# Gated cross-attention block on one core: token and attention-output tiles transposed by DMA instead of TensorE

## The chip, the cores and the metric

The kernel runs on one core of a Trainium2 chip. The metric is the time of the device in microseconds for one execution. A core has the engines PE (TensorE), DVE (VectorE), ACT (ScalarE), POOL (GpSimd) and SP (SyncE); each works through its own instructions in order, and semaphores tie them together.

## The reference

Two batches of 2048 tokens with 512 features go through gated cross-attention (16 heads of 32 features, 77 context positions) and a gated feed-forward block with fake-quantised activations and weights (hidden size 1408):

```python
q = (layernorm(x) @ Wq)                      # heads of 32
scores = q @ k.T * scale ; attn = softmax(scores)
x = x + tanh(g_xattn[0]) * ((attn @ v) @ Wo)
xq = act_fake_quant(layernorm(x), clip_x)    # needs max |layernorm(x)| over all tokens
h  = act_fake_quant(silu(xq @ wg) * (xq @ wu), clip_down)
x = x + tanh(g_ffn[0]) * (h @ wd)
```

Only the attention part is touched here.

## The kernel before

The 4096 tokens are 32 tiles of 128 (NT = 32), held in `x1`. The kernel has three blocks one after the other: attention (up to about 406 us), "up" and "down". In the attention block all engines walk the same slots n = 0 to 35 (`tile_slots`, L326), and in a slot several tiles at different steps are in hand. Slots 4 to 19 are a hardware loop, the rest is written out. Every engine's work stands in a fixed order written out by hand in its `slot`, and only semaphores tie the engines together, so an instruction that waits holds up all that stands behind it on its engine.

Tile m is handled in this order:

- POOL's `deviation` (L423) turns mean and variance into scale and bias; ACT's `normalise` (L494) writes the normalised tile `xn` (one buffer).
- PE's `x_transpose` (L885) turns `xn` into `p_x` with four 128x128 f32 transposes. ACT copies the high part to `xT_hi` (L503), DVE the rest to `xT_lo` (L611).
- PE's `queries` (L892) and `scores` (L912, two halves). DVE takes the row maximum (L633) and subtracts it into `prob` (L639); this write of half 0 is called the first subtraction here, that of half 1 the second. ACT takes the exponential (L531). `prob` has two buffers, for even and odd tiles, with 616 f32 elements in each half.
- PE transposes the probabilities in three groups (L937), ACT copies each group (L527), PE multiplies with the values (L948), DVE divides by the sum into `o_sb` (L652), half by half.
- In slot m+2 PE's `out_transpose` (L963) turns `o_sb` into `p_x` with four transposes, ACT and DVE split it into `oT_hi` (L515) and `oT_lo` (L662), and at the end of the slot `project` (L974) multiplies with Wo into `p_y`, DVE adds to `x1` in slot m+3 (L730) and takes statistics. In slot m+4 ACT writes the absolute value of the second layernorm to `xabs` (L522), and DVE takes its maximum (L782).

Beside this runs the preparation of the feed-forward weights: in slots 0 to 21 one row block a slot is loaded by SP (`rows`, L349), DVE takes its maximum (L753), scales it to int8 (L771), POOL casts it to bf16 (L458), and SP issues one DMA transpose of 128x512 two-byte elements (`rows_transposed`, L344). From slot 22 on the down weights go a similar way.

PE's order in slot n, for the steps that matter: scores half 0 of tile n, `out_transpose(n-2)`, eight probability transposes of tile n-1, queries, outputs half 0, scores half 1, two probability transposes, queries, outputs half 1, `x_transpose(n+4)`, `project(n-2)`. ACT ends its slot with the exponential of half 1, the copy to `xT_hi` of tile n+4, and `normalise(n+5)`.

## Time and profile before

| | us |
|---|---|
| median of 3 runs | 651.65 (651.65 to 651.79) |
| the profiled execution | 651.6 |
| its span from first to last instruction | 649.6 |

The profile comes from one execution. "Busy" counts an instruction from its start to its end; instructions of one engine overlap a little, so the distance from one start to the next (called the pitch here) is what the engine's order costs. Line numbers are those of the kernel before.

### The profile page before, as it was taken

The page shows a single profiled execution, that of the slowest core. Times are in us where ns is not written, and L with a number is a line of the kernel's source. Part 1 is how long each engine was busy: PE and PEld are TensorE (multiplying, and loading weights), DVE is VectorE, ACT ScalarE, POOL GpSimd, SP SyncE. Part 2 cuts the span into 40 slices and gives each one's busy share as a digit, 9 for nine tenths or more (in the row PEclk, how much of TensorE's full clock was granted, in tenths as well). Part 3 has the DMA queues.
Part 4 walks back from the last instruction along what each step waited for, and adds up shares of the span by engine and source line. Part 5 has one row for each costly group of instructions (what it writes and reads, how often), then busy time and mean ns, then how long its engine had stood idle before and what let it go on. Part 6 is the DMA issues. An engine that isn't in the chain of part 4 may idle for free. (4 is left out here: it accounts for less than half of the span.)

```text
span 649.6 us, 12819 instructions
## 1 busy us (share of the span) xinstructions
PE 629.0 (97%) x3987; PEld 478.6 (74%) x4008; DVE 505.3 (78%) x954; ACT 319.8 (49%) x488; POOL 174.5 (27%) x392
## 2 busy tenths in 40 slices
PE   8969999999999999999999997899999999899997
PEld 6769999999999999999999997444444444344544
DVE  6686878788787887888888766688888888876764
ACT  4354544445444554544544432555555554365653
POOL 7121223223232222212212111111111110047775
PEclk9999999999999999999999999899999999999999
DMA  8639111101111011011112000058465110089723
GB/s 308 189 95 318 47 28 26 49 24 48 24 29 44 25 48 25 28 52 62 29 47 68 18 7 0 18 174 192 161 210 202 31 28 17 0 291 413 292 105 128
DMA packets 59861, 63.32 MB, mean 97 GB/s; under 512 B 39571, under 2 KB 42029, under 8 KB 59821
## 3 DMA queue, kind: packets, MB, share of 16 engines
q1 hardware_dynamic: 54915, 46.03, 23.7%
q10 hardware_dynamic: 4906, 16.78, 7.0%
q8 instruction: 22, 0.36, 0.2%
q14 instruction: 18, 0.15, 0.1%
HBM read 32.48 MB, written 21.36 MB: 83 GB/s over the span
## 5 line engine op out<-in xcount | busy, mean ns | idle before, releaser
L633 DVE TENSOR_REDUCE sb_smax<-ps_s 128x8 f32<-128x616 f32 x64 | 51.1, 799 | 59.4 <-PE ps_s L926 59.0
L1231 ACT ACTIVATE sb_silu<-ps_g,sb_sgu 128x512 f32<-128x512 f32 x88 | 60.5, 687 | 72.1 <-PE ps_g L1318 43.8
L1318 PE MATMUL ps_g<-sb_xqT,sb_wgu 128*128 128x512 bf16 x344 | 89.3, 379 | 1.0 <-DVE sb_xqT L1274 0.6
L1318 PE MATMUL ps_u<-sb_xqT,sb_wgu 128*128 128x512 bf16 x346 | 89.4, 379 | 0.3
L527 ACT COPY sb_pT<-ps_p 128x512 f32<-128x512 f32 (+1 forms) x96 | 46.5, 520 | 71.5 <-PE ps_p L937 71.5
L1289 DVE SCALAR_TENSOR_TENSOR sb_h<-ps_u,sb_sgu,sb_silu 128x512 f32<-128x512 f32 (+1 forms) x88 | 66.1, 751 | 19.4 <-PE ps_u L1318 18.8
L948 PE MATMUL ps_o<-sb_vblk,sb_pT 128*128 (+4 forms) x640 | 79.0, 270 | 1.2 <-ACT sb_pT L527 1.2
L948 PEld LDWEIGHTS ps_o<-sb_vblk,sb_pT 128*128 128x128 f32 (+1 forms) x640 | 76.8, 191 | 1.8 <-ACT sb_pT L527 1.4
L881 PE MATMUL ps_q<-sb_xT_hi,sb_wq_hi 128*128 128x256 f32 x256 | 78.0, 305 | 0.0
L882 PE MATMUL ps_q<-sb_xT_lo,sb_wq_hi 128*128 128x256 f32 x256 | 72.6, 284 | 0.0
L883 PE MATMUL ps_q<-sb_xT_hi,sb_wq_lo 128*128 128x256 f32 x256 | 72.6, 284 | 0.0
L1524 PE MATMUL ps_z<-sb_wdT,sb_hq 128*128 128x512 bf16 x324 | 71.2, 379 | 0.3
L1399 POOL TENSOR_TENSOR sb_wgu<-sb_wgu,sb_x 128x512 f32<-128x512 f32 x31 | 53.4, 1723 | 52.3 <-DVE sb_wgu L1456 52.0
L1293 DVE TENSOR_REDUCE sb_hmax<-sb_h 128x1 f32<-128x512 f32 (+1 forms) x88 | 60.4, 686 | 8.0 <-DVE sb_h L1289 0.7
L1318 PEld LDWEIGHTS ps_g<-sb_xqT,sb_wgu 128*128 128x128 bf16 x352 | 34.4, 98 | 42.1 <-ACT sb_xqT L1245 0.8
L1318 PEld LDWEIGHTS ps_u<-sb_xqT,sb_wgu 128*128 128x128 bf16 x352 | 34.4, 98 | 41.5
L515 ACT CAST sb_oT_hi<-ps_x 128x512 fp32r<-128x512 f32 x31 | 18.2, 587 | 90.2 <-PE ps_x L971 90.2
L1524 PEld LDWEIGHTS ps_z<-sb_wdT,sb_hq 128*128 128x128 bf16 x330 | 32.2, 98 | 39.0 <-ACT sb_hq L1416 0.5
L1419 ACT CAST sb_hq<-sb_h 128x1408 bf16<-128x1408 int8 (+1 forms) x32 | 42.0, 1312 | 27.5 <-DVE sb_h L1449 23.6
L639 DVE TENSOR_TENSOR sb_prob<-ps_s,sb_smax 128x616 f32<-128x616 f32 x64 | 51.0, 796 | 2.7
L440 POOL TENSOR_TENSOR sb_ve<-sb_mvt,sb_eps 128x1 f32<-128x1 f32 x32 | 6.1, 190 | 172.1 <-DVE sb_mvt L757 170.3
L881 PE MATMUL ps_y<-sb_wo_hi,sb_oT_hi 128*128 128x512 f32 x124 | 51.3, 414 | 0.0
(212 smaller groups left out, 1351.8 us busy)
## 6 DMA issues: line engine op xcount, KB each, us to landing
h_spill<-sb_h SPq DMA_DIRECT2D x4, 2816.0 KB, 8.9
sb_h<-h_spill ACTq DMA_DIRECT2D x16, 704.0 KB, 7.5
out_dram<-sb_wgu SPq DMA_DIRECT2D x31, 256.0 KB, 2.1
sb_x<-in_x_dram ACTq DMA_DIRECT2D x1, 4096.0 KB, 16.8
sb_w_in<-in_L_ffn_w_gate_dram SPq DMA_DIRECT2D x11, 256.0 KB, 2.6
sb_w_in<-in_L_ffn_w_up_dram SPq DMA_DIRECT2D x11, 256.0 KB, 2.6
sb_x<-in_x_dram SPq DMA_DIRECT2D x2, 1024.0 KB, 14.7
sb_x<-in_x_dram SPq DMA_DIRECT2D x2, 512.0 KB, 5.3
```

Source lines behind the costliest of these rows:

```text
L633: dve.tensor_reduce(smax[:, half, :].rearrange("p (g h) -> p g h", g=2), half_scores(), X, ALU.max).then_inc(v_max, 1)
L639: dve.tensor_tensor(prob[t % 2][:, half, :].rearrange("p (g h m) -> p g h m", g=2, h=HG), half_scores(), smax[:, half, :].rearrange("p (g ...
L881: pe.matmul(o, hi, rhi, start=first, stop=False)
L882: pe.matmul(o, hi, rlo, start=False, stop=False)
L883: return pe.matmul(o, lo, rhi, start=False, stop=last)
L948: last = pe.matmul(p_o[:, first:end + 1, :].rearrange("p h d -> p (h d)"), pT[rows, half * KB + j, :], vblk[rows, span(b), half, SLOT0[j]: ...
L1231: act.activation(silu[(j * KI + i) % 2][:, :, :].rearrange("p t n -> p (t n)"), p_g[(j * KI + i) % 2][:, :], ACT.Silu, scale=sgu[:, i:i + ...
L1289: dve.scalar_tensor_tensor(steps_h, p_u[(j * KI + i) % 2][:, :, :], sgu[:, KI + i:KI + i + 1], silu[(j * KI + i) % 2][:, :, :], ALU.mult, ...
L1293: dve.tensor_reduce(hmax[:, span(u)], steps_h, mybir.AxisListType.XY, ALU.max, apply_absolute_value=True).then_inc(v_hmax, 1)
L1318: last = pe.matmul(banks[(j * KI + i) % 2][:, :], wgu[:, what, k, i * P:(i + 1) * P], xqT[j][:, k, :], start=(k == 0), stop=(k == KD - 1))
L1399: pool.tensor_tensor(yd[k], yd[k], x1[:, span((v + RT) % NT), :].rearrange("p a d -> p (a d)"), ALU.add).then_inc(g_out, 1)
L1524: last = pe.matmul(p_z[k % 4][:, :], hq[k % 4][:, i, :], wdT[:, i, :], start=(i == 0), stop=(i == KI - 1))
```

## The change

Tiles 8 to 31 of the normalised tokens and tiles 2 to 29 of the attention output are no longer transposed by PE. POOL splits each f32 tile, seen as pairs of 16-bit halves, into a plane of low and a plane of high halves; SP transposes the planes by DMA (two-byte elements); ACT joins the transposed planes into f32 words in a buffer `xpl`, and copies from there to the high part. The planes are written into `prob`, which is idle for that time: those of the token tile in half 1, those of the output in half 0. So the next subtraction into a half of `prob` waits until the DMA that reads its planes has landed. `xabs` moves to the PSUM bank of `p_y` for most tiles, because `xpl` takes its place, and `project` waits for its maximum. DVE's order within a slot is changed. Some semaphores are shared between blocks to make room for the new ones.

```diff
@@ SP: once a slot
+                    def planes_transposed(n):
+                        sp.wait_ge(g_xpl, n - DIRECT + 1)
+                        sp.dma_start_transpose(xn_u[:, :].rearrange("p (c n) -> p c n", n=P),
+                                               x_planes(n)).then_inc(d_xT, 16)
+                    def out_transposed(m, half):
+                        sp.wait_ge(g_opl, 2 * (m - O_FIRST) + half + 1)
+                        sp.dma_start_transpose(o_pairs(half).rearrange("p (c n) -> p c n", n=P),
+                                               o_planes(m, half)).then_inc(d_oT, 16)
+                    def slot_transposes(n):
+                        if o_joined(n - 2):
+                            out_transposed(n - 2, 1)
+                        if DIRECT <= n + 4 < NT:
+                            planes_transposed(n + 4)
+                        if o_joined(n - 1):
+                            out_transposed(n - 1, 0)
@@ POOL
+                    def x_split(t):
+                        pool.tensor_copy(x_planes(t).rearrange("p (two n) -> p two n", two=2), xn_pairs)\
+                            .then_inc(g_xpl, 1)
+                    def out_split(t, half):
+                        pool.tensor_copy(o_planes(t, half).rearrange("p (two n) -> p two n", two=2),
+                                         o_pairs(half).rearrange("p (n two) -> p two n", two=2)).then_inc(g_opl, 1)
+                    def deviation(n, t, x_ready=False, o_ready=False):
                         wait(pool, v_st, n + 1)
                         wait(pool, g_nb, n)
-                        wait(pool, a_xn, n - 1)
+                        if x_ready:
+                            wait(pool, a_xn, n)
+                            wait(pool, t_p, 3 * (n - 6))
...
+                        if o_ready:
+                            wait(pool, v_o, 2 * (n - 6))
                         pool.tensor_tensor(ve[:, :], mv[:, 1:2], eps[:, :], ALU.add).then_inc(g_self, 1)
                         pool.tensor_tensor(nmean[:, :], mv[:, 0:1], minus[:, :], ALU.mult).then_inc(g_self, 1)
+                        if o_ready:
+                            out_split(t - 7, 1)
+                        if x_ready:
+                            x_split(t - 1)
                         wait(pool, g_self, 3 * n + 2)
...
-                    def deviation2(m):
+                    def deviation2(m, t):
...
+                        if o_joined(m + 2):
+                            wait(pool, v_o, 2 * (m + 2) + 1)
+                            wait(pool, t_p, 3 * (m + 2) + 2)
                         pool.tensor_tensor(nb2[:, span(m)], nmean2[:, :], rs2[:, span(m)], ALU.mult)\
                             .then_inc(g_nb2, 1)
+                        if o_joined(m + 2):
+                            out_split(t + 2, 0)
@@ ACT
+                            wait(act, a_xpl, n - DIRECT)          # normalise
+                    def out_join(m):
+                        wait(act, d_oT, 32 * (m - O_FIRST + 1))
+                        wait(act, v_xlo, min(m + 6, NT) if isinstance(m, int) else m + 6)
+                        act.copy(xpl_halves, o_halves).then_inc(a_opl, 1)
+                        wait(act, a_opl, m - O_FIRST + 1)
+                        wait(act, t_y, m)
+                        act.copy(oT(m)[0], xpl_T).then_inc(a_ohi, 1)
+                    def x_join(n, t):
+                        wait(act, d_xT, (n - DIRECT) * 16 + 16)
+                        wait(act, v_olo, n - 5)
+                        act.copy(xpl_pairs, xn_planes).then_inc(a_xpl, 1)
+                        wait(act, a_xpl, n - DIRECT + 1)
+                        wait(act, t_q, n - t % 2 - 2)
+                        act.copy(xT_hi[t // 2][:, :, t % 2 * P:(t % 2 + 1) * P], xpl_T).then_inc(a_xhi, 1)
...
                         for c, (k0, k1) in enumerate(CHUNKS):
+                            if c == 2 and runs(n - 2, NT) and o_joined(n - 2):
+                                out_join(n - 2)
...
+                            if half == 0 and runs(n - 4, NT - 1):     # between the two exponentials
...
+                                act.activation(xabs(n - 4), row(n - 4), ACT.Abs, bias=nb2[:, span(n - 4)],
+                                               scale=rs2[:, span(n - 4)]).then_inc(a_abs, 1)
@@ DVE
+                        if half == 0 and o_joined(n - 2):             # in scores_sub
+                            wait(dve, d_oT, 32 * (n - 1 - O_FIRST))
+                        if half == 1 and runs(n + 4, NT) and joined(n + 4):
+                            wait(dve, d_xT, 16 * (n + 5 - DIRECT))
@@ PE
+                        if not isinstance(m, int) or m < PLANES_FREE - 2:   # project
+                            wait(pe, v_xmax, m)
-                        if runs(n - 2, NT - 1):
+                        if runs(n - 2, NT - 1) and not o_joined(n - 2):
                             out_transpose(n - 2)
-                        if runs(n + 4, NT):
+                        if not joined(n + 4):
                             wait(pe, v_olo, n - 1)
                             x_transpose(n + 4)
```

(`DIRECT` is 8, `O_FIRST, O_END` are 2 and 30; the remarks behind # stand for the function that the line is in.) DVE's new order in slot n is: maximum half 0, add to `x1`, maximum of the weight rows, first subtraction, statistics, reciprocal, division half 0, `out_part(n-2)` (the write of `oT_lo`), maximum half 1, int8 scaling, maximum of `xabs`, second subtraction, then as before but with `stats_end` ahead of `x_part`. Before, the write of `oT_lo` and the weight maximum stood between the statistics and the reciprocal, and the maximum of `xabs` behind the second subtraction.

## Rows read from the trace of the kernel before

**Rows 1.** The page, its head and part 1 (busy us, share of span, instructions)

```profile
span 649.6 us, 12819 instructions
...
PE 629.0 (97%) x3987; PEld 478.6 (74%) x4008; DVE 505.3 (78%) x954; ACT 319.8 (49%) x488; POOL 174.5 (27%) x392
```

**Rows 2.** Busy time by stretch: us, busy per engine, PEclk, DMA share, GB/s

```profile
200.00:300.00 100.00, 100.00 (x753) 95.59 (x752) 83.74 (x180) 51.29 (x89) 25.78 (x84) 1.00 0.12 34
```

**Rows 3.** Timeline of PE around slot 16: start us, us, operation

```profile
206.11 0.60 PE L889 MATMUL ps_x<-sb_identf,sb_xn 128*128 128x128 f32 x4
206.47 0.48 PE L881 MATMUL ps_y<-sb_wo_hi,sb_oT_hi 128*128 128x512 f32 x1
...
209.33 0.30 PE L924 MATMUL ps_s<-sb_k_hi,sb_q_hi 128*128 x1
...
210.18 0.60 PE L971 MATMUL ps_x<-sb_identf,sb_o_sb 128*128 128x128 f32 x4
210.61 1.04 PE L937 MATMUL ps_p<-sb_identf,sb_prob 128*128 128x128 f32 x8
...
213.95 0.39 PE L924 MATMUL ps_s<-sb_k_hi,sb_q_hi 128*128 x1
...
220.83 0.30 PE L924 MATMUL ps_s<-sb_k_hi,sb_q_hi 128*128 x1
```

**Rows 4.** Timeline of DVE in slot 16

```profile
211.92 0.80 DVE L639 TENSOR_TENSOR sb_prob<-ps_s,sb_smax 128x616 f32<-128x616 f32 x1
...
213.23 0.68 DVE L662 TENSOR_TENSOR sb_oT_lo<-ps_x,sb_oT_hi 128x512 fp32r<-128x512 f32 x1
213.82 0.68 DVE L753 TENSOR_REDUCE sb_w_am<-sb_w_in 128x1 f32<-128x512 f32 x1
214.41 0.17 DVE L757 BATCH_NORM_AGGREGATE sb_mvt<-sb_bn 128x2 f32<-128x6 f32 x1
...
215.09 0.80 DVE L633 TENSOR_REDUCE sb_smax<-ps_s 128x8 f32<-128x616 f32 x1
...
216.20 0.80 DVE L639 TENSOR_TENSOR sb_prob<-ps_s,sb_smax 128x616 f32<-128x616 f32 x1
216.91 0.68 DVE L782 TENSOR_REDUCE sb_xmax<-sb_xabs 128x512 f32 x1
...
221.88 0.80 DVE L633 TENSOR_REDUCE sb_smax<-ps_s 128x8 f32<-128x616 f32 x1 [1.94 <-PE ps_s L926]
```

**Rows 5.** Timeline of ACT in slot 16

```profile
212.33 0.84 ACT L522 ACTIVATE sb_xabs<-sb_x,sb_nb,sb_rs 128x512 f32 x1
215.31 0.38 ACT L527 COPY sb_pT<-ps_p 128x256 f32<-128x256 f32 x1 [2.15 <-PE ps_p L937]
215.58 0.72 ACT L531 ACTIVATE sb_prob<-sb_prob 128x616 f32<-128x616 f32 x1
...
218.73 0.82 ACT L497 ACTIVATE sb_xn<-sb_x,sb_nb,sb_rs 128x512 f32 x1
```

**Rows 6.** Timeline of POOL around slot 16

```profile
205.23 0.61 POOL L458 CAST sb_w_bf<-sb_w_i 128x512 bf16<-128x512 int8 x1
208.61 0.19 POOL L429 TENSOR_TENSOR sb_ve<-sb_mv,sb_eps 128x1 f32<-128x1 f32 x1 [2.77 <-DVE sb_mv L598]
...
209.02 0.55 POOL L432 TENSOR_TENSOR sb_rs<-sb_ve,sb_mhalf 128x1 f32<-128x1 f32 x1
```

**Rows 7.** DMA issues: count, KB each, median us from issue to landing

```profile
wd_spill<-sb_w_bf SPq DMA_DIRECT2D x8, 128.0 KB, 1.7
...
sb_wgu<-sb_w_bf SPq DMA_TRANSPOSE x22, 2.5
...
sb_wdT<-wd_spill SPq DMA_TRANSPOSE x4, 3.7
```

**Rows 8.** Instruction groups of ACT from 560 to 650 us, shapes apart

```profile
L1419 ACT CAST sb_hq<-sb_h 128x1408 bf16<-128x1408 int8 x30 | 41.0, 1365 | 27.5 <-DVE sb_h L1449 23.6 <-PE ps_z L1524 3.9
L1416 ACT CAST sb_hq<-sb_h 128x512 bf16<-128x512 int8 x4 | 2.4, 616 | 5.7 <-DVE sb_h L1446 5.7
```

More of the change, by code:

```diff
@@ L11 @@
 U8 = mybir.dt.uint8
+U16 = mybir.dt.uint16
 ACT = mybir.ActivationFunctionType
@@ L308, in wait, with o_joined, joined @@
                         eng.wait_ge(sem_, value)
+                def o_joined(m):
+                    return not isinstance(m, int) or O_FIRST <= m < O_END
+                def joined(n):
+                    return not isinstance(n, int) or n >= DIRECT
                 def last_tile(m):
@@ L495, in normalise @@
                         wait(act, g_nb, n + 1)
-                        wait(act, t_x, n)
+                        if isinstance(n, int) and n <= DIRECT:
+                            wait(act, t_x, n)
+                        else:
+                            wait(act, a_xpl, n - DIRECT)
                         act.activation(xn[:, :], x1[:, span(n), :].rearrange("p a d -> p (a d)"), ACT.Identity,
@@ L518, in slot @@
                         for c, (k0, k1) in enumerate(CHUNKS):
-                            if c == 2 and runs(n - 4, NT - 1):
-                                wait(act, g_nb2, n - 3)
-                                wait(act, v_xmax, n - 3)
-                                act.activation(xabs[:, :], row(n - 4), ACT.Abs, bias=nb2[:, span(n - 4)],
-                                               scale=rs2[:, span(n - 4)]).then_inc(a_abs, 1)
+                            if c == 2 and runs(n - 2, NT) and o_joined(n - 2):
+                                out_join(n - 2)
                             if runs(n - 1, NT):
@@ L535, in slot @@
                         if runs(n + 4, NT):
-                            x_part(n + 4, t)
+                            if joined(n + 4):
+                                x_join(n + 4, t)
+                            else:
+                                x_part(n + 4, t)
                         if runs(n + 5, NT):
@@ L765, in slot @@
                             outputs_norm(n - 1, 0)
+                        if runs(n - 2, NT - 1) and o_joined(n - 2):
+                            out_part(n - 2)
                         if runs(n, NT):
@@ L773, in slot @@
                         down_part(n, 1)
+                        if runs(n - 4, NT):
+                            wait(dve, a_abs, n - 3)
+                            dve.tensor_reduce(xmax[:, span(n - 4)], xabs(n - 4), X, ALU.max).then_inc(v_xmax, 1)
                         if runs(n, NT):
@@ L779, in slot @@
                                               ALU.subtract).then_inc(v_wo, 1)
-                        if runs(n - 4, NT):
-                            wait(dve, a_abs, n - 3)
-                            dve.tensor_reduce(xmax[:, span(n - 4)], xabs[:, :], X, ALU.max).then_inc(v_xmax, 1)
                         down_part(n, 2)
@@ L798, in slot @@
                             stats(n + 6)
+                        if runs(n + 6, NT):
+                            wait(dve, v_bn, n + 7)
+                            wait(dve, g_nb, n + 5)
                         if runs(n - 1, NT):
@@ L996, in slot @@
                             scores(n, t, 0)
-                        if runs(n - 2, NT - 1):
+                        if runs(n - 2, NT - 1) and not o_joined(n - 2):
                             out_transpose(n - 2)
```

118 lines of the change are left out of this document (84 added, 34 removed).

## The prediction

> **What bounds the kernel now.** I read the page first: PE is busy for 97% of the span, DVE for 78%, ACT and POOL for half and a quarter [rows 1]. Such a share can hide stages with another limit, so the busy time by stretch comes next: between 200 and 300 us, in the middle of the attention block, PE is busy for the whole 100 us at the full granted clock, and DVE for 83.7 [rows 2]. The timeline of PE then gives the slot: the first score product of slot 16 starts at 209.33 and that of slot 17 at 220.83, so a slot takes 11.50 us, with no gap [rows 3]. DVE ends every slot with an idle time of 1.94 us that a score product ends [rows 4]; 11.50 - 1.94 = 9.56 us is its work. So in the attention block PE sets the pace, and what leaves PE shortens the slot only as long as DVE's 9.56 us, and every chain of waits that closes on itself from slot to slot, stay below the new slot.
>
> **What PE is spared.** The four transposes of an attention output cost PE 210.61 - 210.18 = 0.43 us, the four of a token tile 206.47 - 206.11 = 0.36 us [rows 3]. These are distances from start to start, which is what counts on a full engine. Without both a slot of PE is 10.71 us. Over 28 output tiles and 24 token tiles that is 12.0 + 8.6 = 20.7 us, if nothing else takes over. DVE would still fit: 9.56 in 10.71.
>
> **What is added, engine by engine.** Per slot POOL gets two copies of 512 16-bit elements a row and one of 1024; SP three DMA transposes beside the one that it has; ACT two joins of 1024 16-bit elements. None of them is in the trace, so each is bounded. POOL: a cast of 512 elements took 0.61 us [rows 6]; the copy of a half has as many, and I take 0.61. At least it is one of POOL's smallest instructions, 0.19 us, and at most I allow twice 0.61. The token split is then about 1.2. ACT: 512 elements took 0.616 us and 1408 took 1.365 [rows 8], which is 0.84 ns an element and 1.04 us for 1024; the bounds are 0.72 us, the exponential of only 616 elements [rows 5], and the 1.365. The copy behind the join goes from SBUF, 0.62 us by the 512-element row, where the one from PSUM that it replaces is hidden already. DMA: a transpose of 128x512 two-byte elements landed 2.5 us after its issue, and one of 128x1408 took 3.7 [rows 7]; half an output is the first size, so 2.5 us, and the token planes lie between, about 3.2. Busy time is no trouble: ACT's share rises from half to some seven tenths, POOL's stays below six tenths. The new work costs nothing by its amount; it costs by where it waits.
>
> **The weight loads** are issued behind the new transposes in SP's queue, but a slot ahead of their use; I cost them at nothing, covered by that slot.
>
> **The ring.** Follow the first subtraction of slot n. It may write half 0 of `prob` only once both output planes of tile n-2 have landed. The second of these planes is split by POOL in `deviation`, behind a wait for `a_xn`, that is, for ACT's `normalise` at the very end of slot n-1. And that `normalise` stands behind the token join, which stands behind the exponential of half 1, which needs the second subtraction of slot n-1, which follows the first one in DVE's order. So there is a chain from one slot's first subtraction to the next one's, whatever PE does. Its pieces:
>
> 1. From the end of `normalise` to the split: wait and two tiny instructions, about 0.35 (the pow that follows them starts 0.41 behind [rows 6]); the split 0.61. Together 0.96.
> 2. DMA transpose of the half, issue to landing: 2.5 [rows 7].
> 3. From the first to the second subtraction. By DVE alone: subtraction and statistics 213.23 - 211.92 = 1.31; aggregate, reciprocals and division 215.09 - 214.41 = 0.68; `oT_lo` 213.82 - 213.23 = 0.59, which now stands here; maximum and int8 scaling 216.20 - 215.09 = 1.11; maximum of `xabs` another 0.59, as the reduction of that length at 213.82: sum 4.28 [rows 4]. But there is a longer way round over PE and ACT: subtraction 0.80 [rows 4], then score products and two probability transposes until ACT's copy, 215.31 - 213.95 = 1.36 [rows 3, 5], that copy 0.27 and the exponential 0.72, `xabs` 0.84 (moved behind it) [rows 5], its maximum 0.59: sum 4.58. I take 4.6.
> 4. Second subtraction 0.80, exponential 0.72, join 1.04, copy to the high part 0.62, `normalise` 0.82 [rows 4, 5, 8]: 4.0.
>
> Sum 0.96 + 2.5 + 4.6 + 4.0 = 12.06 us. That is more than the 10.71 that PE needs, and 0.55 more than the slot before. DVE's maximum of the weight rows, which the change puts ahead of the first subtraction, fills the wait there but shortens nothing of the ring.
>
> **The sum.** The ring is closed where token tiles are joined, slots 4 to 27: 23 steps from one first subtraction to the next, 23 x 0.55 = +12.7 us. In slots 28 to 31 only the output transposes go, at most 4 x 0.43 = -1.7. Against the profiled execution's own 651.6 us that makes 662.6; the median of the runs is 651.65, the same. I forecast **663 us**.
>
> **A rule on the transfers.** The trace has transposes at 2.5 us and plain stores of 128 KB, the same amount of data, at 1.7 [rows 7]. The Trainium skill (Advanced Engine Details and Errata, X-Bar Transpose) says that transposes on this chip are as fast as regular DMAs. The trace does not agree, 2.5 against 1.7, though the rows differ in their target (SBUF and HBM). By that rule the second piece would be 1.7.
>
> **A rule on a shared port.** At most one input of DVE's two splitting subtractions was in SBUF before (0.68 us with the other in PSUM [rows 4]); now both are. The Trainium skill (SBUF — State Buffer, Who interferes with whom) says that such an instruction and a GpSimd instruction that reads SBUF block one another. No row here shows the two together. In my schedule they miss each other: POOL splits while DVE takes the maximum of half 0 and adds to `x1`.
>
> **Rivals.**
>
> A. *The ring is shorter than the old slot* and the kernel gets faster. It decides at a ring of 11.50 us, 0.56 less than my sum. For it: three of the pieces are estimates. With the lowest bounds, split 0.19, join 0.72 and the way over DVE alone, 4.28, the ring is 12.06 - 0.42 - 0.32 - 0.30 = 11.0, and the time 651.6 - 23 x 0.5 - 1.7 = 638. Against it: the two copies are priced by rows with as many elements or on a straight line through two rows, so both would have to be well under their likeliest. Some middle value gives 645.
>
> B. *A transpose between SBUF tiles lands as quickly as a plain store.* Then piece 2 is 1.7, the ring 11.26, and the time 651.6 - 23 x 0.24 - 1.7 = 644. Against it stand 22 transposes with a median of 2.5 [rows 7], also from SBUF to SBUF.
>
> C. *PE stays the bound*, the waits being hidden by a slot structure that I misread: 10.71 us a slot, 651.6 - 20.7 = 631.
>
> D. *POOL's splits are slowed*, by strided 16-bit reading or by DVE's subtractions of two SBUF operands. If one such subtraction of 0.68 us holds up the output split in each slot, the ring is 12.74 and the time 651.6 + 23 x 1.24 - 1.7 = 678. With the split at twice 0.61 it is nearly the same.
>
> E. *The change does less than it says*: if hardly any transpose left PE the time would be within 0.2% of before. The diff takes them out of PE's order plainly, so I give this only what a ring that happens to equal 11.50 deserves too.
>
> **Chances.** My ring at 12.06, or up to 0.5 above it or 0.3 below: 0.53. D: 0.09. Same, with E: 0.05. A: 0.20. B: 0.06. C: 0.07. A measurement of this kernel can tell a difference of about 0.2%, 1.3 us. So slower 0.62, same 0.05, faster 0.33. The likeliest case alone has the range 654 to 674. For 8 in 10 I must reach down through A and B, to 638, which leaves C and a little of A outside, and up to 676, a ring of 12.65, which leaves most of D outside.
>
> **What would show it.** In the profile of the changed kernel: the distance between the first score products of neighbouring slots (12.06, or 10.71 if C); an idle time of DVE ahead of the first subtraction that a DMA transpose of an output plane ends, 1 to 2 us in every slot; idle time of PE in front of the second half's scores, ended by DVE's first subtraction, about 1 us; POOL's `deviation` released by ACT's `normalise`; the output split at 0.61, the join at 1.04, the landing at 2.5, each a term of the ring. The four transposes L889 and L971 must be gone from slots 4 to 31. I am wrong if DVE does not wait in front of the first subtraction, or if POOL's splits start well before `normalise` of the previous slot has ended; and only the size is off if the ring is there with another length.

## The result, and the profile after

The changed kernel takes 690.98 us (median of 4 runs, 689.99 to 693.47) beside 651.65 us for the kernel before (4 runs on the same chip): a ratio of 1.061, 95% interval 1.058 to 1.064. It is 39 us slower, where the forecast was 11 to 12 us slower and the upper end of the range was 676. The page of the changed kernel, head and part 1, and two of its groups:

```profile
span 688.2 us, 12751 instructions
...
PE 628.1 (91%) x3800; PEld 470.0 (68%) x3800; DVE 512.8 (75%) x954; ACT 391.4 (57%) x540; POOL 237.1 (34%) x472
...
L773 DVE TENSOR_TENSOR sb_prob<-ps_s,sb_smax 128x616 f32<-128x616 f32 x64 | 50.7, 793 | 49.1 <-DMA sb_o_sb<-sb_prob 49.0
...
L614 ACT COPY sb_xpl<-sb_o_sb 128x1024 uint16<-128x1024 uint16 x28 | 37.6, 1343 | 54.5 <-DMA sb_o_sb<-sb_prob 54.5
```

Line numbers are those of the changed kernel from here on. Against [rows 1], PE has 187 fewer matmul records (the transposes taken off are 208), and yet its busy time fell by only 0.9 us, to 628.1: over the fourteen slots 8 to 21 it fell from 160.8 us to 154.9, which is 0.42 us a slot of the 0.79 forecast, and in slots 4 to 7, partly at half clock (see below), it rose from 46.0 to 48.1. Its share fell because the span grew. The row of L773, the first step of the softmax, is the one to read: DVE waited 49.0 us in front of it for the DMA that transposes an output half. Before, no DMA stood there. The middle of the attention block by stretch (us, busy time of PE, PE's weight load, DVE, ACT and POOL, granted clock, DMA share, GB/s):

```profile
200.00:300.00 100.00, 87.74 (x619) 81.56 (x619) 76.84 (x160) 67.64 (x96) 42.20 (x104) 1.00 0.35 77
```

PE was busy for 100 of these 100 us before [rows 2]. No engine is full now, which is what a ring of waits looks like. The waits between 62 and 440 us (total, times, longest) name its links:

```profile
POOL sb_ve L509 <- ACT sb_xn L597: 67.1, 18, 4.9
ACT sb_xpl L614 <- DMA sb_o_sb<-sb_prob: 54.5, 24, 4.3
DVE sb_prob L773 <- DMA sb_o_sb<-sb_prob: 49.0, 24, 4.5
...
PE ps_s L1064 <- DVE sb_prob L773: 35.7, 24, 3.5
```

DVE waits for the DMA, the DMA for POOL's split, POOL for ACT's `normalise`, and ACT, by way of the second subtraction, for DVE. One turn of it, slot 16 to 17, in the timelines of DVE, ACT, POOL and SP:

```profile
227.15 0.80 DVE L773 TENSOR_TENSOR sb_prob<-ps_s,sb_smax 128x616 f32<-128x616 f32 x1 [1.77 <-DMA sb_o_sb<-sb_prob]
...
231.88 0.79 DVE L773 TENSOR_TENSOR sb_prob<-ps_s,sb_smax 128x616 f32<-128x616 f32 x1
...
239.76 0.80 DVE L773 TENSOR_TENSOR sb_prob<-ps_s,sb_smax 128x616 f32<-128x616 f32 x1 [1.73 <-DMA sb_o_sb<-sb_prob]
```

```profile
232.70 0.72 ACT L648 ACTIVATE sb_prob<-sb_prob 128x616 f32<-128x616 f32 x1 [1.06 <-DVE sb_prob L773]
233.32 1.34 ACT L622 COPY sb_xpl<-sb_xn 128x1024 uint16<-128x1024 uint16 x1
234.70 0.62 ACT L625 CAST sb_xT_hi<-sb_xpl 128x512 fp32r<-128x512 f32 x1
235.23 0.81 ACT L597 ACTIVATE sb_xn<-sb_x,sb_nb,sb_rs 128x512 f32 x1
```

```profile
236.37 0.19 POOL L509 TENSOR_TENSOR sb_ve<-sb_mv,sb_eps 128x1 f32<-128x1 f32 x1 [3.89 <-ACT sb_xn L597]
236.51 0.19 POOL L510 TENSOR_TENSOR sb_nmean<-sb_mv,sb_minus 128x1 f32<-128x1 f32 x1
236.63 0.61 POOL L494 COPY sb_prob<-sb_o_sb 128x512 uint16<-128x512 uint16 x1
```

```profile
237.27 1.19 SPq L398 DMA_TRANSPOSE sb_o_sb<-sb_prob  x1
```

Read as the four pieces of the prediction: first to second subtraction 231.88 - 227.15 = 4.73; on to the end of `normalise`, 236.04 - 231.88 = 4.16; on to the end of the split, 237.24 - 236.04 = 1.20; on to the next first subtraction, which the landing releases, 239.76 - 237.24 = 2.52. The sum is 12.61 us. It must equal the slot, being the way from one first subtraction to the next; what makes it a ring is that at each handover the next engine has been waiting: ACT 1.06 us for the second subtraction, POOL 3.89 for `normalise`, DVE 1.73 for the transpose. The same length returns from slot 8 to slot 22, fourteen times over (126.33 to 302.74 us). Before it was 11.49.

**Where the 38.6 us of the two profiled spans arose**, from the starts of the first subtractions in both timelines. Up to slot 4: -0.8. Slots 4 to 28 lasted 311.1 us for 275.8: +35.3, of which the ring explains 24 x (12.61 - 11.49) = 26.9; slots 4 to 8 took 53.08 where four turns make 50.44, +2.6; slots 22 to 28 took 81.64 where six make 75.66, +6.0. Slots 28 to 31: +1.9. Behind slot 31: +2.1.

**The late slots** differ in what is ahead of the transposes. SP's and DVE's timelines there:

```profile
352.24 0.45 SPq L463 DMA_DIRECT2D sb_vblk<-in_L_ffn_w_down_dram  x1
352.74 0.74 SPq L463 DMA_DIRECT2D sb_w_in<-in_L_ffn_w_down_dram  x1
353.52 1.20 SPq L398 DMA_TRANSPOSE sb_o_sb<-sb_prob  x1
```

```profile
357.52 0.80 DVE L773 TENSOR_TENSOR sb_prob<-ps_s,sb_smax 128x616 f32<-128x616 f32 x1 [3.77 <-DMA sb_o_sb<-sb_prob]
```

Right behind three loads of `w_down`, 704 KB in all, the transpose let DVE go 4.0 us after its issue (357.52 - 353.52), not 2.5, and DVE waited 3.77 us, not 1.7. It was issued 0.04 us after POOL's split had ended, so here it is the landing that is late and not the issue; only in front of slot 28 did the issue, too, come 1.3 us behind the split. Beside the loads, piece 3 (first to second subtraction) took 5.1 us in slots 22 to 25, for 4.7 before: DVE reduces and scales the rows of `w_down` in between. That is about 1.6 us of the 6.0.

**PE's clock** takes a share of the excess of slots 4 to 8. Stretches of the changed kernel (columns as above; the granted clock is third from the end), and PE's timeline where it resumes:

```profile
98.00:100.00 2.00, 0.62 (x6) 0.48 (x5) 1.25 (x2) 1.25 (x1) 0.00 (x0) 1.00 0.73 135
100.50:103.50 3.00, 3.00 (x16) 2.96 (x15) 2.21 (x5) 1.91 (x4) 2.49 (x7) 0.50 0.00 0
...
332.00:335.00 3.00, 3.00 (x19) 3.00 (x17) 3.00 (x8) 1.81 (x5) 2.34 (x6) 0.57 0.01 3
...
385.00:390.00 5.00, 4.67 (x21) 4.67 (x22) 4.57 (x11) 2.90 (x5) 2.45 (x6) 0.50 0.00 0
```

```profile
99.69 0.41 PE L1064 MATMUL ps_s<-sb_k_hi,sb_q_hi 128*128 x1 [1.38 <-DVE sb_prob L773]
...
228.09 0.40 PE L1064 MATMUL ps_s<-sb_k_hi,sb_q_hi 128*128 x1 [1.37 <-DVE sb_prob L773]
...
331.09 0.38 PE L1064 MATMUL ps_s<-sb_k_hi,sb_q_hi 128*128 128x308 f32 x1 [2.77 <-DVE sb_prob L773]
```

After an idle time of 2.77 us the grant fell to 0.50, the level of 1.2 GHz, for some 3 us; after 1.38 us at 98 it did so too, and after 1.71 in the next slot, but after 1.37 us at 227 it did not. In the kernel before PE was busy for the whole of the same stretches (85 to 112 us and 310 to 384), at 1.00. What decided that 1.4 us was too much there and not later stays open; in run 6 below the grant stayed at 1.00 after a gap of 2.46 us in slot 7.

What the half clock costs can be read by comparing runs. In slots 6 and 7 piece 3 took 5.23 and 5.59 us; in run 6, which is the same kernel until after its last tile and had full clock there, it took 4.72 and 4.71. That is 1.4 us of the 2.6. Another 1.0 is a single transpose, which landed 3.49 us after its issue in front of slot 7's first subtraction (3.5 to 4.1 in runs 3, 4 and 6 at the same place; why stays open), and 0.3 is piece 3 of slot 4. In slot 24 the half clock cost nothing that can be seen: the slot took 12.96 us, as it did at full clock in run 4.

### The profile page after: what moved, and what is told of

Same layout as the page of the kernel before. It is cut to its first block and busy times, and to the rows that moved or that the text cites. A ratio compares the mean times of both kernels' runs of the same rounds, so it can differ in the third digit from the quotient of the medians.

```text
span 688.2 us, 12751 instructions
## 1 busy us (share of the span) xinstructions
PE 628.1 (91%) x3800; PEld 470.0 (68%) x3800; DVE 512.8 (75%) x954; ACT 391.4 (57%) x540; POOL 237.1 (34%) x472
## 5 line engine op out<-in xcount | busy, mean ns | idle before, releaser
L773 DVE TENSOR_TENSOR sb_prob<-ps_s,sb_smax 128x616 f32<-128x616 f32 x64 | 50.7, 793 | 49.1 <-DMA sb_o_sb<-sb_prob 49.0
L1021 PE MATMUL ps_q<-sb_xT_hi,sb_wq_hi 128*128 128x256 f32 x256 | 79.9, 312 | 0.0
L1088 PEld LDWEIGHTS ps_o<-sb_vblk,sb_pT 128*128 128x128 f32 (+1 forms) x640 | 78.4, 195 | 1.8 <-ACT sb_pT L644 1.4
L1064 PE MATMUL ps_s<-sb_k_hi,sb_q_hi 128*128 128x308 f32 (+1 forms) x128 | 43.2, 338 | 39.3 <-DVE sb_prob L773 37.6
L1022 PE MATMUL ps_q<-sb_xT_lo,sb_wq_hi 128*128 128x256 f32 x256 | 74.5, 291 | 0.0
L1023 PE MATMUL ps_q<-sb_xT_hi,sb_wq_lo 128*128 128x256 f32 x256 | 74.5, 291 | 0.0
L614 ACT COPY sb_xpl<-sb_o_sb 128x1024 uint16<-128x1024 uint16 x28 | 37.6, 1343 | 54.5 <-DMA sb_o_sb<-sb_prob 54.5
L648 ACT ACTIVATE sb_prob<-sb_prob 128x616 f32<-128x616 f32 x64 | 46.1, 721 | 33.6 <-DVE sb_prob L773 33.5
```

What stands on the lines that cost most here:

```text
L773: dve.tensor_tensor(prob[t % 2][:, half, :].rearrange("p (g h m) -> p g h m", g=2, h=HG), half_scores(), smax[:, half, :].rearrange("p (g ...
L1021: pe.matmul(o, hi, rhi, start=first, stop=False)
L1022: pe.matmul(o, hi, rlo, start=False, stop=False)
L1023: return pe.matmul(o, lo, rhi, start=False, stop=last)
L1088: last = pe.matmul(p_o[:, first:end + 1, :].rearrange("p h d -> p (h d)"), pT[rows, half * KB + j, :], vblk[rows, span(b), half, SLOT0[j]: ...
```

## The experiments

All are edits of the changed kernel; runs 5, 11 and 12 build on run 1, and run 9 on run 5. "Slot" is the distance between the first subtractions of neighbouring slots, read from slots 8 to 20 of DVE's timeline unless said otherwise.

**1. The output split ahead of the wait.** In `deviation` POOL waits for `normalise` only in front of what needs it:

```diff
-                            wait(pool, a_xn, n)
                             wait(pool, t_p, 3 * (n - 6))
...
-                        pool.tensor_tensor(nmean[:, :], mv[:, 0:1], minus[:, :], ALU.mult).then_inc(g_self, 1)
                         if o_ready:
                             out_split(t - 7, 1)
                         if x_ready:
+                            wait(pool, a_xn, n)
+                        pool.tensor_tensor(nmean[:, :], mv[:, 0:1], minus[:, :], ALU.mult).then_inc(g_self, 1)
+                        if x_ready:
                             x_split(t - 1)
```

> In the changed kernel POOL's split of the second output plane stands behind the wait for ACT's normalise; here it stands ahead of that wait (only the token split waits for it), nothing else differs. Theory of the ring (first subtraction, second subtraction, exponential, token join, normalise, output split, DMA transpose, first subtraction; 12.6 us measured): the ring is opened, the split can start when the division of half 1 is done, about 1.9 us earlier. The next longest chains are PE's own 10.7 us and DVE's order behind the copy to the high part, so the loop slots come down to about 11.0 us, DVE waits for no output transpose in slots 6 to 21, and the time is near 645 us (640 to 652), under the kernel before. Rival 1, the transposes themselves or the added copies are too much work for the slot: the slot stays above 12.2 us and the time above 680. Rival 2, only a part of the wait goes because the second way round (token planes, second subtraction) is nearly as long: slot 11.8 to 12.2, time 665 to 680.

Measured: 663.74 us (4 runs, 659.57 to 667.13), ratio 1.020 (1.016 to 1.024) to the kernel before. The slot is 11.0 us (10.86 to 11.16). POOL's timeline of slot 16:

```profile
214.11 0.61 POOL L494 COPY sb_prob<-sb_o_sb 128x512 uint16<-128x512 uint16 x1
215.19 0.19 POOL L513 TENSOR_TENSOR sb_nmean<-sb_mv,sb_minus 128x1 f32<-128x1 f32 x1 [0.46 <-ACT sb_xn L598]
```

The split now starts before `normalise` has ended, and in slots 8 to 20 DVE no longer waits for a DMA. One wait, moved, gave back 27 us, so the ring is the cause of the larger part. The time missed the expected 640 to 652 all the same. It is not the whole: slots 21 to 28 still took 11.5 to 15.1 us, with waits for the DMA of up to 4.2. Their sum is 16.7 us over eight slots of 11.0, which is most of the 18.7 by which my 645 missed.

**2. Half the token join.** ACT's join L622 copies only the first half of its elements; the rest of the tile keeps stale data.

> ACT's token join copies only the first half of each plane (512 of 1024 elements), the rest of the tile is left stale; nothing else differs. Theory of the ring: the token join is a piece of the ring, its 1.34 us become about 0.7 to 0.8, and each of the 18 loop slots and the 5 after them gets shorter by the same 0.6: slot 12.0, time 691 - 14 = 677 (675 to 679). Rival, ACT's joins only fill idle time: no change, 690 to 692.

Measured: 679.4 us (one run, as all below for which no number of runs is given), slot 12.02. The join, from ACT's groups by shape:

```profile
L622 ACT COPY sb_xpl<-sb_xn 128x512 uint16<-128x512 uint16 x24 | 18.2, 760 | 0.0
```

1.34 became 0.76, 0.58 less, and the slot fell by 0.59. The join is on the ring in full.

**3. Half the output join**, the same cut in L614 (POOL clears the other half once).

> ACT's output join copies only the first 512 of 1024 elements, the other half of the output tile is left stale (a memset of the buffer is added at the start); nothing else differs. It has the same cost as the token join of the run beside it (1.34 us) but stands beside the ring: behind it the third copy of transposed probabilities waits for PE anyway. Theory of the ring: slot 12.5 to 12.6, time 688 to 691. Rival, the sum of ACT's work or the wait for the output planes on ACT is the limit: as much gain as from the token join, 677.

Measured: 688.57 us, slot 12.61 as before. The output join lost the same 0.58 us (1.343 to 0.765) and the slot did not move: it is the same kind of instruction, once a slot like the other, but beside the ring. Runs 2 and 3 together show that position, not busy time, is what is paid.

**4. Small down loads.** From its second block on each load of `w_down` takes 16 columns (the first block stays whole, and the rest of the weights is stale):

```diff
                             cols = wd_cols(q)
+                            if r:
+                                cols = slice(cols.start, cols.start + 16)
```

> The loads of the down weights of row blocks 1 to 3 (704 KB each) bring only 16 columns of each piece, the rest of the weights is stale; nothing else differs. In the changed kernel the first subtraction of slots 24, 26 and 28 waits 3.8 to 4.5 us instead of 1.75 and its output transpose, issued right behind three such loads, lands 4 to 5 us after its issue instead of 2.5. Theory: the loads ahead of it in the same queue make it late, so these waits return to about 1.8, 2 to 2.7 us saved each, time about 685 (683 to 687). Rival, the waits come from POOL, which waits for the store of the down weights before the split: no change, 690 to 692.

Measured: 683.09 us. Slots 22 to 27 took 12.98, 12.99, 12.96, 13.29, 11.45 and 13.56 us, where they had taken up to 15.4, and the waits for the DMA there were 2.3 to 2.6 us for up to 4.5. Their sum is 77.23 us for 81.64, so the loaded bytes make 4.4 of the 6.0 us of late excess; the other 1.6 is about what DVE's work on these rows adds, which stays (piece 3 at 5.1 us). The other 3.5 us that this run gained lie mostly outside these slots, and it does not tell why.

**5. The early split, outputs by DMA only up to tile 19.** Run 1 with one constant changed, so that no output is transposed by DMA while `w_down` loads:

```diff
-O_FIRST, O_END = 2, NT - 2
+O_FIRST, O_END = 2, 20
```

> The early output split of the first experiment (loop slots 11.0 us there against 11.5 before), and beside it the outputs are transposed by DMA only for tiles 2 to 19; from tile 20 on PE transposes them again. Theory: the loop slots stay at 11.0; from slot 22 on, where the down weights load DVE, SP and the DMA queues, no output plane has to land before the first subtraction, the token ring (normalise, split 1.04, DMA about 3.4, second subtraction, exponential, join, normalise) is only about 9.3 us long, and PE with the output transposes back needs 11.14; slots 22 to 27 come to 11.1 to 11.5 instead of the 13.3 of the first experiment. Time 651.6 - 17 x 0.5 - 1 = 642 (639 to 646), a version faster than both. Rival, the late slots are long for another reason (POOL waits for the down stores and the token planes are late in turn): slots 22 to 27 stay above 12.3 and the time is above 650.

Measured: 647.25 us (5 runs, 645.64 to 647.97), ratio 0.994 (0.991 to 0.996): 0.6% faster than the kernel before, and the lowest median of the study. The slot is 11.0 us, and 11.39 from slot 22 on, without a wait for a DMA. In 200 to 300 us:

```profile
200.00:300.00 100.00, 98.79 (x713) 93.04 (x712) 88.65 (x182) 71.99 (x106) 44.40 (x110) 1.00 0.36 82
```

My 642 was 5 us too low; the slots came out as expected in both stretches (11.0, and 11.1 to 11.5), so the miss lies outside them and in the spread of the runs.

**6. The price of a copy by its form.** After its last slot ACT makes three more copies, twice each: 1024 16-bit elements in sequence (L725), the same number in steps of two on both sides (L727), 512 32-bit elements (L730).

> The changed kernel with six more ACT copies behind its last tile, twice each: 1024 16-bit elements from and to consecutive places, 1024 16-bit elements with both sides taken in the order of all low then all high halves (steps of two elements), 512 f32 elements; they copy what nobody reads. The join took 1.34 us, and 0.76 with half of the elements, 1.14 ns an element, where the int8 to bf16 cast took 0.84. Theory A, the step of two elements in the write costs: consecutive about 1.04, stepped 1.34 or more. Theory B, it is the 16-bit integer form that is slow, whatever the order: all of 1024 elements at 1.34. Either way 512 f32 at about 0.62. The time of the whole kernel is of no interest (up to 8 us more).

```profile
L727 ACT COPY sb_prob<-sb_prob 128x1024 uint16<-128x1024 uint16 x2 | 2.7, 1342 | 0.1
L725 ACT COPY sb_prob<-sb_prob 128x1024 uint16<-128x1024 uint16 x2 | 2.1, 1036 | 0.0
...
L730 ACT COPY sb_prob<-sb_prob 128x512 f32<-128x512 f32 x2 | 1.2, 617 | 0.1
```

In sequence the copy costs the 1.04 us that I had taken from [rows 8]; the step of two makes it 1.34. It is the form that cost 0.3, not the number or the type.

**7. Outputs alone** (token tiles stay on PE):

> One part of the change alone: outputs of tiles 2 to 29 by DMA, all token tiles by PE as before. Theory of the ring: without token planes POOL's deviation asks only for the normalise of a slot earlier and ACT has no token join, so the ring is open; what is left is subtraction, division of half 1, split, DMA transpose, about 10.9 us, and PE needs 11.07. Loop slots 11.0 to 11.3; the late slots stay long behind the down weights (12 to 14 us). Time 650 to 660, about 30 to 40 under the whole change. Rival, the wait for the output planes' landing is a matter of the output part alone: loop slots still above 12.2, time above 670.

Measured: 663.26 us. The expected 650 to 660 was missed. The slot is 10.9 to 11.2 us, except slot 19 with 12.8, before whose end an output transpose issued right behind a weight load and a weight transpose took 4.3 us to land; the slots from 21 on took 12.7 to 15. With no token split POOL does not wait for `normalise` early, and with no join ACT's part is shorter: the ring is open, and PE sets the pace (busy for the whole of 130 to 250 us, as 11.50 less the 0.43 of the output transposes would have it). What is left of the loss is mostly the late slots.

**8. Tokens alone** (outputs stay on PE):

> The other part alone: token tiles 8 to 31 by DMA, all outputs by PE as before. Theory of the ring: the token ring (normalise, split, DMA, second subtraction, exponential, join, normalise) is about 9.3 us, shorter than PE's 11.14, so PE sets the pace: slots 4 to 27 at 11.14 to 11.3, time 651.6 - 24 x 0.3 = 643 to 646. Both parts alone are then near or under the kernel before, and only together do they close the long ring. Rival, the token join's 2 us on ACT and the split on POOL are what made it slow: slots above 12, time above 665.

Measured: 652.86 us, level with before; my 643 to 646 was wrong. The slot is 11.47, not the 11.14 that PE would allow. PE is busy for 118.2 of the 120 us from 130 to 250. Between the products with the values and `project`, where the token transposes stood, it now waits. The kernel before, then this run:

```profile
216.55 1.22 PE L948 MATMUL ps_o<-sb_vblk,sb_pT 128*128 128x66 f32 x10
217.61 0.60 PE L889 MATMUL ps_x<-sb_identf,sb_xn 128*128 128x128 f32 x4
217.97 0.48 PE L881 MATMUL ps_y<-sb_wo_hi,sb_oT_hi 128*128 128x512 f32 x1
```

```profile
226.48 1.22 PE L1088 MATMUL ps_o<-sb_vblk,sb_pT 128*128 x10
227.88 0.47 PE L1021 MATMUL ps_y<-sb_wo_hi,sb_oT_hi 128*128 128x512 f32 x1 [0.18 <-DVE sb_xmax L916]
```

From the first of these products to `project` it was 1.42 us with the four transposes in between, and it is 1.40 without them: `project` now waits for DVE's maximum of `xabs`, a wait that the change itself added. So taking the token transposes off PE gave back next to nothing (11.47 for 11.50). DVE waits too, in front of `xT_lo`:

```profile
254.09 0.69 DVE L741 TENSOR_TENSOR sb_xT_lo<-sb_xpl,sb_xT_hi 128x512 fp32r<-128x512 f32 x1 [0.87 <-ACT sb_xT_hi L625]
```

From that wait I took a second ring, without a DMA: from `xT_lo` to the second subtraction, over the exponential, the join and the copy to the high part to the next `xT_lo`. That such a way adds up to 11.47 proves nothing, since it runs from an instruction to the same one a slot later; run 9 tests it. Each part of the change alone costs nothing in the middle slots (11.47, and 11.0 to 11.2 but for slot 19), and only both together make 12.61.

**9. The join ahead of the second exponential**, on top of run 5:

```diff
                         for half in range(2):
+                            if half == 1 and runs(n + 4, NT) and joined(n + 4):
+                                x_join(n + 4, t)
```

> The version with the early output split and outputs by DMA for tiles 2 to 19 (loop slots 11.0 us, slots 22 to 29 at 11.39), and beside it ACT's token join and the copy to the high part stand ahead of the exponential of half 1 instead of behind it. Theory: what holds those slots is a second ring without any DMA in it: the write of xT_lo, DVE's slot up to the second subtraction (6.9 us in the loop), its 0.79, the exponential 0.63, the join 1.38, the copy 0.62. With the join ahead of the exponential it runs in ACT's idle time of 1.04 us before that exponential, DVE's 0.87 us of waiting for the high part goes, and the slots come to what PE and its wait for the maximum of xabs leave, 10.7 to 10.95 in the loop and 11.15 to 11.3 after it. Time 2 to 5 us under the version without it: 642 to 645. Rival, PE or DVE's own work holds these slots: no change, 646 to 648.

Measured: 648.69 us (12 runs, 645.12 to 650.46), ratio 0.996 (0.994 to 0.997). The slot stayed at 11.0 to 11.26: no gain over run 5, and the rival stands, PE's or DVE's own work. DVE no longer waits in front of `xT_lo` in any of these slots, so the second ring is open, and DVE waits for PE's scores instead, 10.1 us in 11 slots from 130 to 250 us:

```profile
218.06 0.80 DVE L764 TENSOR_REDUCE sb_smax<-ps_s 128x8 f32<-128x616 f32 x1 [0.78 <-PE ps_s L1067]
```

PE is busy for 118.0 of these 120 us, as in runs 1 and 5, and its one wait in each slot is again the 0.18 us in front of `project`. So by the waits it is PE, with this one in front of `project`, that sets the pace in the middle slots of runs 1, 5, 8 and 9. From slot 22 on runs 5, 8 and 9 all take 11.39, wherever the join stands. What the slot would be without the wait for the maximum was not tested. The output half has little to spare as well: DVE waits 0.15 to 0.35 us for it in 9 slots between 130 and 300 us.

**10. The same join, moved, in the changed kernel itself.**

> The changed kernel with nothing but ACT's token join and the copy to the high part moved ahead of the exponential of half 1; POOL's split stays behind the wait for normalise. Theory of the long ring: it has been opened on POOL in the first experiment; here it is made shorter on ACT, where join and copy (1.38 + 0.53 us) no longer lie between that exponential and normalise. The ring is 12.6 - 1.9 = 10.7 and something else takes over between 10.9 and 11.5; loop slots 10.9 to 11.5, the waits for output planes 0 to 0.6 us, time 691 - 1.1 to 1.7 x 22 = 654 to 667. Rival, what made the first experiment fast was POOL's or SP's earlier start as such: slots stay above 12.2, time above 682.

Measured: 672.99 us, slot 11.44, waits for the DMA 0.56 to 0.60. The ring's fourth piece loses the join and the copy behind it, 1.96 us, and the ring falls by 1.17, from another side than in run 1. The rest is probably given back by the second exponential, which now waits for ACT to finish them: in the changed kernel ACT had only 1.06 us of idle time in front of it. Slots 21 to 28 took 11.4 to 16 us, and the whole missed the expected 654 to 667 by them.

**11. Run 1 with the small down loads of run 4.**

> The kernel with the early split of the outputs, with all output transposes, and with the loads of w_down cut to 16 columns a piece from the second row block on (the down weights are then stale data of the right size; every other instruction stays, so the time is read for the queue alone). With full loads this version took 663.7 us and its steps 21 to 27 took 12.7, 12.5, 14.3, 12.7, 14.5, 11.5, 15.1 us, where the steps before them took 11.0. Theory: what those steps lose is the landing of the output planes behind the 704 KB of down loads. Then steps 21 to 27 come to 11.4 to 12 us each, their waits for a DMA fall below 1 us, and the time is 648 to 655. Rival: the down rows' other work (DVE's reductions and scalings, POOL's casts, the stores) lengthens the ring by itself. Then the steps stay at 12.5 or more and the time is 660 to 664.

Measured: 657.83 us (4 runs, 656.67 to 658.13), between theory and rival in time, while most slots are the rival's (12.5 or more). Slots 21 to 27 took 13.26, 12.51, 12.71, 12.50, 13.28, 11.26 and 13.59 us, so the bytes are 5.9 us of the time by the medians (4.1 in these slots of the profiled runs), and something else remains, 12 us over slots of 11.0. One part is the place in SP's queue:

```profile
317.97 1.19 SPq L398 DMA_TRANSPOSE sb_o_sb<-sb_prob  x1
319.21 3.03 SPq L471 DMA_DIRECT2D wd_spill<-sb_w_bf  x2
322.28 0.43 SPq L465 DMA_DIRECT2D sb_w_in<-in_L_ffn_w_down_dram  x1
322.76 0.45 SPq L465 DMA_DIRECT2D sb_vblk<-in_L_ffn_w_down_dram  x1
323.25 1.01 SPq L465 DMA_DIRECT2D sb_w_in<-in_L_ffn_w_down_dram  x1
324.31 1.20 SPq L398 DMA_TRANSPOSE sb_o_sb<-sb_prob  x1
```

POOL's split of that half ended at 322.58 (L496, 321.97 and 0.61). Its transpose was issued 1.73 us later, because three loads, however small, stood ahead of it in SP's queue, themselves held back by two stores until 322.28. In front of slots 24 and 28 it was 1.2 and 1.3 us. Slot 21 (13.26) is the first block of `w_down`, whose loads are whole in this run: the transpose right behind them landed 4.9 us after its issue. In slots 22 and 24 neither is to blame: the transpose was issued at once and landed in 2.6 us, and yet they took 12.5. There the split came late, 9.3 us behind the first subtraction for 8.0 in slot 16. DVE's statistics, for which POOL then waits, ended at 8.6 instead of 7.7 us, behind the reductions and scalings of the down rows. And POOL's small instruction ahead of the split met DVE's `xT_lo` (284.49 to 285.18):

```profile
284.60 0.63 POOL L510 TENSOR_TENSOR sb_ve<-sb_mv,sb_eps 128x1 f32<-128x1 f32 x1 [4.18 <-DVE sb_mv L731]
```

It took 0.63 us, for 0.19 in the middle slots. So the rival, the other work of the down rows, holds for these two slots, and adds a POOL instruction that DVE holds up.

**12. Run 1 with the loads behind the transposes** of output half 1 and of the token tile, at their full size. This holds from the second block on; the first block's loads stay ahead:

```diff
                             planes_transposed(n + 4)
+                        if down is not None:
+                            down_rows(down)
                         if o_joined(n - 1):
```

> The kernel with the early split of the outputs and all output transposes, with full down loads, but SP issues the three loads of a down row block behind the transposes of output half 1 and of the token tile, no longer ahead of them. In the run with small down loads the steps 21 to 27 stayed at 11.3 to 13.6 us (time 657.8), and SP's timeline showed the output transposes issued 1.2 to 2.3 us after the split, because two stores (3.0 us) and three loads (0.4 to 1.0 us each) stood ahead of them. Theory: the place in SP's queue, with the landing behind the loaded bytes, is what those steps lose. Then the transposes are issued within 0.3 us of the split, land 2.5 us later, steps 21 to 27 come to 11.0 to 11.8 us each, and the time is 644 to 650. Rival 1: the bytes, wherever they are issued, disturb the transposes of the next half: steps of 12 to 13 us, 654 to 660. Rival 2: the down weights now come too late for DVE, which waits for a load in front of the maxima of its rows, and the time is 655 or more by that wait.

Measured: 661.66 us (6 runs, 659.04 to 665.08), ratio 1.017 (1.013 to 1.020). It is rival 2. The waits between 300 and 385 us:

```profile
DVE sb_wd_am L807 <- DMA sb_w_in<-in_L_ffn_w_down_dram: 8.0, 3, 4.2
DVE sb_smax L764 <- PE ps_s L1067: 6.5, 4, 1.9
DVE sb_prob L774 <- DMA sb_o_sb<-sb_prob: 5.0, 4, 2.1
```

DVE's wait for the output planes fell from 13.7 us (run 1, same stretch) to 5.0, as the theory has it, and 8.0 us of waiting for the down weights took its place. Slots 21 to 27 took 13.1, 12.5, 11.6, 16.7, 12.3, 15.2 and 13.0. The first two are near those of run 1, and slot 21 is again the first block (a landing of 4.75 us). In the others the loads and the output planes need the same queue at the same moment, and whichever goes second makes DVE wait.

## Why the prediction was right in direction and wrong in size

- **The ring** was right, link by link: who waits for whom, the wait in front of the first subtraction (1.7 us; 1 to 2 was said), PE's idle time in front of the scores (1.37; about 1), POOL released by `normalise`. Runs 1, 2 and 10 shorten it at two of its pieces and run 3 cuts an instruction beside it, and only the former move the slot.
- **The transposes' landing** (piece 2) was 2.52 for 2.5. Rival B, with a plain store's 1.7, is out in the middle slots. Rival C (PE stays the bound) and E are out by the waits above. Rival A's shorter ring is out too, and with the ring open the slot was 11.0 us and not the 10.71 that the sum for PE has: the wait for the maximum of `xabs` in front of `project`, named among the changes, has no place in it.
- **The first step that failed is the ring's length**, and the term mis-sized most is the join in piece 4: 1.34 us for 1.04. The straight line through [rows 8] was right for the count and blind to the step of two (run 6). The upper bound that I had, 1.365, was the better value. Part of it came back in overlaps (4.16 for 4.0).
- **Piece 1** was 1.20 for 0.96: POOL's start and its two small instructions took 0.59, not 0.35. **Piece 3** was 4.73 for 4.6. Together the ring came to 12.61 instead of 12.06, so each turn cost 1.12 over the old slot instead of 0.55: 26.9 us instead of 12.7. A margin of half a microsecond between a ring and a slot doubles with an error of 5% in the ring; that alone makes 14 of the 28 us that I missed, and brings the time to 676 or 677, the upper end of the range. The ring also ran for 24 steps and not 23: slot 4 to 5 was the first. (The lower end of the likeliest case is worked out loosely: a ring 0.3 shorter gives 656, not 654.)
- **The second step that failed** is "The weight loads are issued behind the new transposes in SP's queue, but a slot ahead of their use; I cost them at nothing". It is right for the other weights and wrong for `w_down`: there the code issues the loads ahead of the output half and the token tile. I looked at the weight loads as what might be late. In the late slots it is the other way round: the ring waits for transposes behind the down loads, on the DMA engines first of all (a landing of 4.0 us for 2.5), and, in runs 1 and 11, in SP's queue as well. Slots 22 to 28 cost 6.0 us over the ring, 4.4 for the loaded bytes (run 4) and 1.6 for DVE's work on the down rows, which the prediction does not mention.
- **"Slots 28 to 31: at most -1.7"** was +1.9. Slot 28 still began with a wait of 4.5 us for a transpose, PE ran at half clock behind it, and output transposes taken off PE did not win that back.
- **Slots 4 to 8** cost 2.6 us over the ring: about 1.4 at half clock after gaps of 1.4 and 1.7 us, 1.0 for one late landing, 0.3 in slot 4. The prediction had about 1 us of idle time of PE in every slot and no price for what such a gap does to the clock.
- **Rival D** (a slowed split, 678) gave a time nearer to the result for a wrong reason: the split took 0.614 us as priced (56 of them). Its shared-port half has a trace now, see below: off the ring in the changed kernel, and on it in two late slots of run 11.

## What to carry to other kernels

When an edit adds waits between engines, follow them from one turn of the loop to the next and sum the ring; if it comes within some 5% of the present period, each uncertain term on it decides the result, so take the bound of the nearest form (type, step and place of the operands), not of the nearest size. Then walk the same ring through every stage of the loop that has other traffic: a transfer on the ring must be priced with whatever is ahead of it in its queue in that stage. A wait that guards only the second of two instructions belongs behind the first; that single move gave back 27 of 39 us here. And when an engine is to be relieved, look for waits that the same edit puts into its order: here one of them took the room of the token transposes.

## What the runs showed of the hardware

- **ACT's copy of 16-bit elements in steps of two** took 1.342 us for 1024 elements, in sequence 1.036 (run 6).
- **A transpose's landing depends on its neighbours**: 2.5 us in the middle slots, 4.0 behind 704 KB of loads, 2.6 to 2.8 there with the loads cut to 16 columns (slots 22 to 26 of run 4). The Trainium skill (Advanced Engine Details and Errata, X-Bar Transpose) says that transposes on this chip are as fast as regular DMAs; 2.5 beside 1.7 for a store of the same 128 KB [rows 7] stays the measured difference, though no run here shows a plain copy between the same tiles.
- **DVE and POOL do hold each other up.** POOL's pow in `deviation2` took 0.549 us in the kernel before (11 of them between 130 and 270 us), 0.824 in the changed kernel, where it meets DVE's `oT_lo` with both inputs in SBUF, and 0.551 in run 8, where `oT_lo` reads PSUM again and ends before the pow begins:

```profile
L527 POOL TENSOR_TENSOR sb_rs<-sb_ve,sb_mhalf 128x1 f32 x11 | 9.1, 824 | 2.1 <-POOL sb_nmean L525 2.1
```

```profile
L527 POOL TENSOR_TENSOR sb_rs<-sb_ve,sb_mhalf 128x1 f32 x11 | 6.1, 551 | 1.9 <-POOL sb_nmean L525 1.9
```

  The other way round, `xT_lo` took 0.85 us in the two middle slots of run 1 where it began 0.30 to 0.32 us after POOL's split, 0.74 to 0.75 where it began 0.41 after it, and 0.69 where it began 0.5 after it or met none. The Trainium skill (SBUF — State Buffer, Who interferes with whom) says that a DVE instruction with two SBUF inputs contends with a GpSimd instruction that reads SBUF and that the order of issue decides which one blocks. The traces agree: each time it is the later one that is longer, by 0.14 to 0.15 us less than what was left of the other (pow +0.30 with 0.44 of `oT_lo` left at 141.22 us; `xT_lo` +0.16 with 0.31 of the split left; run 11's L510 above +0.44 with 0.58 left). The prediction had them miss each other, having looked at the splits and not at the small instructions.
- **PE's granted clock** in the changed kernel fell to half after both gaps of 2.8 us, and after 1.4 us in one slot and not in others; in run 6 it stayed full after one of 2.46 us. A spell at half clock cost the ring 0.5 and 0.9 us in slots 6 and 7, 0.75 in slot 10 of run 4 and nothing in slot 24.
